# Expert stage of a two-layer kernel: one early down product between each two gathers, the last pair gathered by wide products, its last one-hots made by ScalarE and VectorE

## What is computed

```python
q = (xn @ w_q.T).reshape(b, s, 2, NH, KD).transpose(2, 0, 1, 3, 4)
sim = jnp.einsum('pbnhd,hkpd->pbnhk', q, keys_p)
scores, idx = jax.lax.top_k(sim, K)
...
sc, pk = jax.lax.top_k(all_scores, K)
indices = jnp.take_along_axis(all_idx, pk, axis=-1)
wd = down[indices]
hmid = jnp.einsum('bnd,bnhkd->bnhk', inputs, wd)
hmid = jax.nn.sigmoid(sc) * jax.nn.gelu(hmid, approximate=False)
wu = up[indices]
return jnp.einsum('bnhk,bnhkd->bnd', hmid, wu)
```

## Time and profile before

| | us |
|---|---|
| median of 3 runs | 570.51 (569.88 to 571.12) |
| the profiled execution | 570.92 |
| its span | 569.2 |
| PE busy | 419.2 (74%), 6612 products |
| VectorE busy | 470.6 (83%) |
| ScalarE busy | 307.4 (54%) |
| GpSimd busy | 182.0 (32%) |

### The profile page before, as it was taken

The page is one execution under the profiler, slowest core; times in us unless marked ns, Lnnn a source line. Parts: engine busy times, 40 slices in busy tenths (PEclk is TensorE's granted clock), DMA queues, the critical chain, the costliest instruction groups (busy, mean ns, idle before and its releaser), DMA issues. The chain is left out here.

```text
span 569.2 us, 16579 instructions
## 1 busy us (share of the span) xinstructions
PE 419.2 (74%) x6612; PEld 298.3 (52%) x6612; DVE 470.6 (83%) x2060; ACT 307.4 (54%) x639; POOL 182.0 (32%) x208
## 2 busy tenths in 40 slices
PE   1768869987999879965754863848588878785574
PEld 1454547654776467633653323646356545555564
DVE  4585878699887988599884699999989999999961
ACT  0601275427652475314640558483968686868580
POOL 4450122944177143833350150303031313130000
PEclk9997979788867977795555785566657576758577
DMA  7220000000000000000000000000000000000000
GB/s 215 64 65 0 1 2 2 1 2 0 1 1 3 0 1 2 2 1 0 1 2 1 1 1 2 5 3 12 3 12 2 13 2 14 2 13 3 13 12 11
DMA packets 12475, 6.98 MB, mean 12 GB/s; under 512 B 3182, under 2 KB 11758, under 8 KB 12398
## 3 DMA queue, kind: packets, MB, share of 16 engines
q1 hardware_dynamic: 10566, 4.34, 2.8%
q10 hardware_dynamic: 1832, 1.58, 0.9%
HBM read 4.87 MB, written 1.05 MB: 10 GB/s over the span
## 5 line engine op out<-in xcount | busy, mean ns | idle before, releaser
L1749 ACT ACTIVATE hot_last<-iota_f,lo_last 128x128 f16<-128x128 f32 x256 | 77.5, 393 | 0.3 <-DVE lo_last L1875 0.3
L2018 PE MATMUL psum<-hot_w,hot_lo 64*128 64x8 f16 x3072 | 45.3, 164 | 30.9 <-issue 20.4
L2018 PEld LDWEIGHTS psum<-hot_w,hot_lo 64*128 64x128 f16 x3072 | 43.0, 100 | 44.2 <-issue 29.1
L1980 PE MATMUL psum<-x3t,down_t 128*128 128x512 f32 x64 | 44.4, 817 | 16.3 <-ACT hid L1714 14.6
L1889 DVE TENSOR_TENSOR hot_lo<-lo_t,iota_lo 128x4096 f16<-128x4096 f16 x24 | 53.5, 2284 | 0.0
L1660 POOL TENSOR_TENSOR eq<-eq,side_f 128x1024 f16<-128x1024 f16 x14 | 29.0, 2088 | 51.5 <-DVE eq L1853 51.5
L1329 PE MATMUL psum<-q_hi,k_t 32*128 32x128 f16 x256 | 36.1, 259 | 8.9 <-DVE masked L905 7.7
L1822 DVE FIND_INDEX8 side_i<-side,keysims 128x8 uint32<-128x32 f32 x256 | 41.5, 185 | 0.0
L1250 PE MATMUL psum<-we,x1t 128*128 128x512 f32 x64 | 40.2, 776 | 0.4 <-DVE z L842 0.4
L1668 POOL TENSOR_TENSOR rstd<-rstd,minus_half 128x2 f32<-128x2 f32 x8 | 5.7, 708 | 108.4 <-DVE rstd L1923 108.4
L584 POOL TENSOR_TENSOR a_rstd<-a_rstd,minus_half 128x2 f32<-128x2 f32 (+1 forms) x12 | 9.6, 804 | 84.5 <-DVE a_rstd L749 84.5
(11 more groups left out here) (271 smaller groups left out, 1162.1 us busy)
## 6 DMA issues: line engine op xcount, KB each, us to landing
xall<-in_L_attn_x SPq DMA_DIRECT2D x4, 256.0 KB, 6.3
out<-o SPq DMA_DIRECT2D x8, 128.0 KB, 2.1
we<-in_L_ffn_We SPq DMA_DIRECT2D x1, 512.0 KB, 4.5
downn<-in_L_ffn_down SPq DMA_DIRECT2D x1, 512.0 KB, 5.5
upw<-in_L_ffn_up SPq DMA_DIRECT2D x1, 512.0 KB, 6.4
wh<-in_L_attn_W_h SPq DMA_DIRECT2D x1, 256.0 KB, 4.6
keysn<-in_L_ffn_keys_p ACTq DMA_DIRECT2D x1, 256.0 KB, 9.7
wqkv<-in_L_attn_w_qkv ACTq DMA_DIRECT2D x1, 192.0 KB
```

The lines of the kernel that those rows point to most:

```text
L1749: ins = nc.scalar.activation(hot_last[:, lane], iota_f[:], ACT.Abs, bias=lo_last[:, lane:lane + 1], scale=-1.0)
L1980: nc.tensor.matmul(bank[H_BANK(b, c)][:], v.down_t[:, c, :], v.x3t[:, N * b:N * b + N], start=True, stop=True).then_inc(h_mm.h, 1)
L2018: ins = nc.tensor.matmul(bank[2 + q // 2 * 2 + t][:, c:c + EH], low, hot_w[half, i, lane // 2, :, lane % 2], start=(lane % (2 * LB) == 0 a ...
```

## The change

**Early down products.** PE's loop over a pair places `hidden` for `early[0]` before gather 0, `early[1]` before gather 1 and `early[2]` before gather 2.

**`weigh` of pairs 0 to 6.** It still makes four multiplications of 512 elements per partition, but each now covers one tile and two quarters (64 lanes) instead of two tiles and one quarter. `outputs(p)` waits for the third of them before tile 0's products and for the fourth before tile 1's, instead of for all four.

**Pair 7, gathers.** A new buffer `hot_wide` is filled with zeros on GpSimd near the start of the stage. In pair 7 DVE writes the weighted high one-hots of tile 0 (partitions 0 to 63) to columns of their own and those of tile 1 (64 to 127) to others, in four multiplications on 64 partitions instead of two on 128. One product over all 128 partitions then gathers a lane of both tiles into 16 columns: 64 products a quarter instead of 128, and one PSUM bank for each quarter. `weigh(7)` waits for each quarter by itself; `outputs(7)` for all four.

**Pair 7, last one-hots.** ACT makes 16 of the last 32 lanes (`ACT_LANES`) and a Relu over half as much. DVE makes the other 16 (`last_lanes`: a subtraction and a one-hot of 2048 elements), in the place of quarter 0 of `hot_lo`, so after PE has gathered that. It stands between `one_hots(7)` and `residual(6)`; the last gather waits for both engines.

```diff
@@ scalar
-                    for lane in range(LB):
+                    for lane in range(ACT_LANES(p)):
...
-                    nc.scalar.activation(hot_last[:], hot_last[:], ACT.Relu, bias=1.0, scale=-1.0)\
-                        .then_inc(hot_last_ok.h, 1)
+                    made = hot_last[:, 0:ACT_LANES(p)]
+                    nc.scalar.activation(made, made, ACT.Relu, bias=1.0, scale=-1.0).then_inc(hot_last_ok.h, 1)
@@ gpsimd
+                nc.gpsimd.memset(hot_wide[:], 0.0).then_inc(zeroed.h, 1)
@@ vector, one_hots
+                    if p == PAIRS - 1:
+                        dve.wait_ge(zeroed.h, 2)
                     for i, w in enumerate((w_hi, w_lo)):
...
+                        for t in range(2):
+                            own_rows = slice(HK * t, HK * t + HK)
+                            ins = nc.vector.tensor_tensor(
+                                hot_wide[own_rows, i, :, t], hot_hi[own_rows],
+                                bc(w[own_rows].rearrange("p (j s) -> p j s", s=2).unsqueeze(2), [HK, P // 2, EH, 2]),
+                                ALU.mult)
...
+                def last_lanes():
+                    rest = slice(P - LB // 2, P)
+                    wait(dve, hot_ok, PAIRS - 1, 1)
+                    wait(dve, g_mm, PAIRS - 1, 1)
+                    step(nc.vector.scalar_tensor_tensor(lo_t[:, 0:LB // 2], hi_t[:, rest], -float(P), number[:, rest],
+                                                        ALU.mult, ALU.add))
+                    nc.vector.tensor_tensor(
+                        hot_lo[:, 0:LB // 4],
+                        bc(lo_t[:, 0:LB // 2].rearrange("p (j s) -> p j s", s=2).unsqueeze(2), [P, LB // 4, P, 2]),
+                        bc(v.iota_lo[:].unsqueeze(1), [P, LB // 4, P, 2]), ALU.is_equal).then_inc(hot_ok.h, 1)
@@ vector, weigh
+                    if p == PAIRS - 1:
+                        for q in range(QB):
+                            wait(dve, g_mm, p, q + 1)
+                            lanes = slice(LB * q, LB * q + LB)
+                            nc.vector.tensor_tensor(
+                                mix[:, :, lanes], bank[2 + q][:].rearrange("p (l e) -> p e l", e=2 * EH),
+                                hid[:, b % 2, at:at + 2, :, lanes].rearrange("p t e l -> p (t e) l"), ALU.mult)\
+                                .then_inc(mix_ok.h, 1)
+                        return
+                    for half in range(2):
+                        wait(dve, g_mm, p, 2 * half + 2)
+                        lanes = slice(2 * LB * half, 2 * LB * half + 2 * LB)
+                        for t in range(2):
+                            nc.vector.tensor_tensor(
+                                mix[:, EH * t:EH * t + EH, lanes],
+                                bank[2 + 2 * half + t][:].rearrange("p (l e) -> p e l", e=EH),
+                                hid[:, b % 2, at + t, :, lanes], ALU.mult).then_inc(mix_ok.h, 1)
@@ tensor, gathered
+                            if p == PAIRS - 1:
+                                at, c = lane - LB * q, 2 * EH * (lane - LB * q)
+                                if q < QB - 1:
+                                    low = hot_lo[:, lane // 2, :, lane % 2]
+                                elif at < ACT_LANES(p):
+                                    low = hot_last[:, at, :]
+                                else:
+                                    low = hot_lo[:, (at - LB // 2) // 2, :, at % 2]
+                                ins = nc.tensor.matmul(
+                                    bank[2 + q][:, c:c + 2 * EH], low,
+                                    hot_wide[:, i, lane // 2, :, :, lane % 2].rearrange("p t e -> p (t e)"),
+                                    start=(i == 0), stop=(i == 1))
+                                continue
@@ tensor, outputs
-                    wait(pe, mix_ok, p)
...
+                        wait(pe, mix_ok, p, 3 + t if p < PAIRS - 1 else QB)
@@ tensor, the loop over pairs
-                    for c in early[0:2]:
-                        hidden(p // PB + 1, c)
-                    gathered(p, 0)
-                    for c in early[2:3]:
-                        hidden(p // PB + 1, c)
-                    for q in range(1, QB - 1):
+                    for q in range(QB - 1):
+                        for c in early[q:q + 1]:
+                            hidden(p // PB + 1, c)
                         gathered(p, q)
```

## The result

The changed kernel takes 566.83 us (median of five executions, 565.86 to 567.86), against 570.73 for the kernel before on the same chip (five executions, 569.88 to 572.60). The ratio is 0.9928, with a 95% interval from 0.9904 to 0.9952: 3.9 us faster, between 2.7 and 5.5. The forecast was 564.8 within a range of 562.4 to 567.6, a gain of 5.75. A second comparison, further down, gave 0.9929 (0.9905 to 0.9953). So the direction, and the place of most of the gain, came as forecast; about two microseconds of it did not.

What follows compares the result with a forecast made beforehand. DVE was taken to set the pace mid-stage and instruction arrival to bound pair 7's gathers. Gains 1.9 + 3.85 = 5.75 from 570.92 give 565.2, and 0.4 less for the median 564.8 us; range 562.4 to 567.6.

Steps and rivals of the forecast that it cites:

- (b): Pairs 3 to 5: ACT's later Relu delays its outputs or keys copy for DVE; 566.7 or 567.7; chance 0.13.
- (c): Pair 7: DVE's four half-height multiplications take 1.2 each, everything from `hot_lo` on 2.5 later: 567.3; chance 0.07.
- Part 1: Early down products spread out, pairs 2 to 5: pair 2 gains 1.65, the others hardly change; 1.9 us in sum.
- the 504.4: Pair 5: a Relu on ACT later than 504.4 would show the forecast wrong; 504.3 was expected.
- so do the instruction blocks, since these bursts now lie 3.8 us apart anyway: PE's gathers, worked for pair 5: arrival of instruction blocks hides under ACT's Relu, with bursts 3.8 us apart.
- Part 2: `weigh` and `outputs` of pairs 0 to 6: same four multiplications, cut differently; nothing gained, bounds 0.7 us.
- Part 3: Pair 7: `hot_lo` starts 1.2 later, `mix` ends at 553.8, output products start 3.85 us earlier.
- (a): Pairs 2 to 5: faster PE clock, each product 1.0 shorter, the remaining 3.3 us of waiting goes: 561.5; chance 0.08.
- (d): Pair 7's gathers: full-height weight loads don't overlap, 102 ns per product, 26.1 us in all: 582.4; chance 0.04.
- (e): Pair 7: fetch stays the bound; blocks needing 5 us start outputs 0.5 later, inside the range; no separate chance.

Runs made afterwards that it cites:

- e6: Changed kernel, but pair 7 gathered by 512 narrow products as before, the last one-hots still shared; 570.10 us, ratio 0.9960 to the kernel before.
- e5: Changed kernel, wide products kept, but ACT makes all 32 one-hots of pair 7's last quarter; 566.26 us, ratio 0.9898 to the kernel before.
- e8: Changed kernel, but early products spread in pair 2 only and a key product of pairs 2 to 5 moved behind the last gather; 572.04 us, ratio 1.0004.
- r1: Changed kernel again without an edit, a second profiled execution; 565.15 us (one execution).
- e2: Changed kernel with the old order of early down products, new tail and new `weigh` kept; 568.27 us, ratio 0.9942 to the kernel before.
- e1: Kernel before with only the early down products moved, old `weigh` and old tail; 569.05 us, ratio 0.9983 to the kernel before.
- r2: Changed kernel without an edit, a third time; 566.63 us, ratio 0.9929 to the kernel before.

## The prediction against the runs, point by point

The measured 566.83 lies inside the range, 2.0 above the forecast and 0.8 below the upper end. The range reached that far for rivals (b) and most of (c). (b) didn't happen and (c) only to a sixth, so that the range held the result is in part its width.

**What bounds the kernel.** That the tail was bound by the arrival of instructions was right, and is shown by e6: without fewer instructions the stops stay and the tail is 18.64, with them it falls to 16.17 (e5) and 15.55. The Trainium skill ("Runtime: NRT & Kernel Launch", section "Instruction fetch mechanics") calls the crossing of a block mostly hidden; e6 and e8, with stops of 1.08 to 2.36 and 1.19 to 2.44 us, contradict that for gathers of small products.

**Part 1, forecast 1.9.** Without a stop the waits of pairs 2 to 5 were 0.94, 1.00, 0.93 and 1.01 in r1, 3.9 in sum where 3.3 was forecast (0.9 and three times 0.8). Pair 2 was right to 0.1 in its number, but not in what it named. The prediction put PE's lateness there down to the order of the products and left out a stop for instructions that its trace already had in gather 2 (kernel before, PE, pair 2):

```profile
414.89 1.25 PE L2018 MATMUL psum<-hot_w,hot_lo 64*128 64x8 f16 x82 [1.32 <-issue]
```

Without this stop the last gather would have started at 418.08 - 1.4 = 416.7 instead of the Relu's 416.3. By this estimate from the rows some 1.4 of the 1.6 us gained in pair 2 come from the stop that is gone, and 0.2 from the earlier start; that the number fits is in part luck. In pairs 3 to 5 the mechanism was right for ACT: PE's gain at the front is lost on it. Its timeline in pair 5 of the changed kernel, which answers to the earlier trace rows:

```profile
494.97 0.60 ACT L1721 ACTIVATE hid<-psum 128x512 f32<-128x512 f32 x1 [1.73 <-PE psum L2020]
495.47 3.02 ACT L1756 ACTIVATE hot_last<-iota_f,lo_last 128x128 f16<-128x128 f32 x10
498.78 0.60 ACT L1721 ACTIVATE hid<-psum 128x512 f32<-128x512 f32 x1 [0.30 <-PE psum L2020]
...
499.99 3.62 ACT L1763 ACTIVATE hot_last<-hot_last 128x4096 f16<-128x4096 f16 x1
```

The Relu begins 11.3 us after the first `hot_lo` of its pair (488.66); before it was 498.56 - 489.49 = 9.1. It is 2.3 later where the forecast had 2.1, and ends at 504.44 by the clock of the old pair 5, just past the 504.4 that the prediction named as a sign of being wrong. The term that was too small is this chain, by 0.2 in each pair, which goes straight into DVE's wait. As a stretch, part 1 is worth 139.59 - 138.2 = 1.4 us against the trace of before, and 2.4 against the other trace of the old order (140.56, e2). So 1.9 was a fair size for an execution without a stop. What failed is the sentence "so do the instruction blocks, since these bursts now lie 3.8 us apart anyway". It holds for five of the seven traces. In the other two the block of pair 3 came 1.8 or 2.35 us late and took the whole of the part's gain (interiors 140.30 and 140.62). The spacing was not what lacked: between gather 2 and the last gather lay a key product and the wait for the Relu, 3.2 us in all. What the sentence left out is that a fetch may start only when PE goes on behind that wait, 1.0 and 0.9 us into the last gather. Over the seven traces the interior averages 138.9 us against 140.1 for the two of the old order, so 1.2 us rather than 1.9.

**Part 2, forecast 0.** No group of `mix` in pairs 2 to 5 takes longer or shorter (1.28 or 1.29 us for two). The interior of e1, with the old `weigh`, is 138.20 us, and those of r1 and r2, with the new one, are 138.22 and 138.19. So nothing to 0.03 us, as forecast.

**Part 3, forecast 3.85, measured 3.47.** The mis-sized term is the four multiplications on 64 partitions. I took the duration to follow the elements of a partition alone, 2.43 in sum. They took from 539.02 to 541.84, 2.82 us, so 0.70 each from start to start instead of 0.61. Since DVE then works without a gap, these 0.39 us arrive undiminished at the outputs; 3.85 - 0.39 is 3.46. All else held: the one-hots of the last 16 lanes 1.15 (1.14 forecast), four `mix` 2.5, wide products 27 ns, ACT done at 542.86 + 1.91 = 544.8, 6.95 us after `lo_last` (6.8 forecast). GpSimd's fill took 3.51 us and was hidden: it had 2.21 us of idle time left behind it.

```profile
326.63 3.51 POOL L1689 MEMSET hot_wide<- 128x4096 f16 x1
332.35 4.13 POOL L1666 TENSOR_TENSOR eq<-eq,side_f 128x1024 f16<-128x1024 f16 x2 [2.21 <-DVE eq L1860]
```

**The rivals.** (a) The faster clock in the interior didn't come: the spread products last 2.0 us for two, as before. (b) ACT's later Relu reached no later step; e8 shows what it looks like when that chain is late. (c) was right in kind and a sixth of its size: 0.39 us, not 2.5. (d), the slower case, is refuted: 27 ns a product, no stop for weight loads, where one load measured 102 ns and those of these products 103 to 104. The Trainium skill ("TensorE: Matmul & The Clock Gate", Part 3, "The mechanism") states the rule behind (d); these products all use the same full rows, and their loads still overlap, so the measurement speaks against it. (e) didn't come: no stop at all was seen among the wide gathers.

**The sum.** 1.2 for part 1 and 3.5 for part 3 give 4.7. The measured gains, 3.9 (2.7 to 5.5) and 4.0 (2.7 to 5.4), hold that; they hold 5.75 no longer. The 0.7 us between 4.7 and 4.0 is within these intervals, and I don't assign it to anything.

**What stays open.** Why the fetches of pair 3 started later in some executions. Other DMA traffic is not the reason. While PE stood in the stopped trace, the store of an output tile moved 73 GB/s, but it began after the late fetch had (the DMA view has none of its packets between 443.9 and 445.4). And r1 moved the same store at the same time (its 82 GB/s hold one packet of instructions too) and ran through. In the view of windows the last three columns are the granted clock, the DMA share and GB/s; first the stopped trace, then r1:

```profile
444.00:445.40 1.40, 1.40 (x102) 1.34 (x102) 0.81 (x2) 0.97 (x3) 1.40 (x2) 0.50 0.06 18
445.40:447.20 1.80, 0.03 (x2) 0.00 (x0) 0.00 (x0) 0.00 (x0) 1.80 (x2) 0.50 0.25 73
```

```profile
445.40:447.20 1.80, 1.80 (x35) 1.18 (x28) 1.33 (x4) 0.00 (x0) 1.80 (x2) 0.50 0.27 82
```

## What to carry to other kernels

Idle time of an engine without any releaser may be the arrival of instructions, but need not be: the 1.2 us before each last gather carry the same label and end with ACT's Relu. So count the instructions between two such gaps. If it is some 255 each time and the distance repeats (here 3.6 to 4.2 us), make fewer and larger instructions rather than earlier data. One long product between two bursts was enough pause here, except where the engine was also held by another engine just ahead of the burst; there the next block was asked for before the wait in some executions and behind it in others. Look at several traces before explaining one of them, and at when the instruction queue's packets start. Before moving an operation that seems to be in the way, such as the key products in e8, look for who reads its result on the other engines.

## What the runs showed of the hardware that was not expected

- A VectorE multiplication of 1024 16-bit elements per partition takes longer on 64 partitions than on 128: 0.70 us from start to start against 0.61 (four in 2.82, two in 1.21). The two forms also differ in the layout of their output, and no run tells which of both costs the 0.09 us.
- The same program, at nearly the same instant (443.90 and 443.96), can run a gather of 128 products in 1.8 us or stop in it for 1.8 us more. The stop lies after 102 products both times that it was seen, as does the shorter one of the kernel before, so the limit's place is fixed and its cost is not. Its block was fetched 3 us before the gather in one case and 1.0 us after its start in the other; the transfer took 0.96 us in both.
- Products with full-height weights (128 rows) and 16 columns follow one another every 27 ns at the lower clock level of 1.2 GHz, while one of their weight loads measures 103 to 104 ns. The products on half the rows with 8 columns take 14 ns (128 in 1.80 us from start to start, also at 1.2 GHz). A product that gathers both tiles thus costs PE nearly the same as two that gather one each (27 against two times 14 ns): halving the instructions saved no execution time at all, only their arrival.
